# A gated relational graph layer: normalising and turning the input tiles inside the first sweep, landing weights from another queue, and splitting u a tile earlier

## The reference

```
h = maximum(layernorm(x), 0)
u = h @ root + bias
for r in range(8):
    sums = segment_sum(h[src] * (type == r), dst);  cnt = segment_sum(type == r, dst)
    u = u + (sums / maximum(cnt, 1)) @ weight[r]
z = concatenate([u, h]) @ w_gate + b_gate
out = x + tanh(u) * z + h * (1 - z)
```

## Time and profile before

| | us |
|---|---|
| median of 3 runs | 1621.51 (1617.54 to 1622.1) |
| the profiled execution's own time | 1619.02 |
| its span | 1617.3 |
| PE busy | 1444.5 |
| DVE busy | 682.4 |
| ACT busy | 345.6 |
| POOL busy | 644.0 |

### The profile page before, as it was taken

How to read it: one execution, slowest core, us unless ns; L and a number is a source line. 1 busy time by engine, 2 the same in 40 slices (tenths; PEclk the granted TensorE clock), 3 DMA queues, 4 the chain that set the end, 5 groups by cost and what they waited for, 6 DMA issues and landing times.

```text
span 1617.3 us, 21089 instructions
## 1 busy us (share of the span) xinstructions
PE 1444.5 (89%) x6978; PEld 777.6 (48%) x6978; DVE 682.4 (42%) x1163; ACT 345.6 (21%) x426; POOL 644.0 (40%) x1021
## 2 busy tenths in 40 slices
PE   1476999789999998999999989999999999897797
PEld 0233454345556444544545544455554455554464
DVE  5314965755564233224323312432332334454555
ACT  6324213110201121121222102212212111222221
POOL 2311000368784445344444434434443445410343
PEclk9877999899999999999999999999999999999898
DMA  4441031102001733544464364364455447411465
GB/s 188 129 155 49 39 142 64 40 27 114 1 1 53 247 120 111 190 150 134 128 231 133 119 216 128 118 232 138 132 175 184 126 133 252 136 53 60 125 200 157
DMA packets 63442, 207.41 MB, mean 128 GB/s; under 512 B 12709, under 2 KB 13084, under 8 KB 63354
## 3 DMA queue, kind: packets, MB, share of 16 engines
q0 software_dynamic: 28224, 81.95, 16.9%
q1 hardware_dynamic: 22458, 78.10, 14.2%
q10 hardware_dynamic: 12672, 46.14, 7.7%
HBM read 170.67 MB, written 56.32 MB: 140 GB/s over the span
## 4 chain that ended last, share of the span: by engine, by line
PE 75%; DVE 8%; DMA 5%; issue 4%; ACT 3%; POOL 2%; SPq 1%; ACTq 0%; POOLq 0%; DVEq 0%
PE ps L932 61%; PE ps L873 10%; DMA reg<-y_rows,idx 3%; DMA W<-in_x_dram 2%; PE ps L861 2%; DVE W L587 1%; PE ps L863 1%; DVE W L702 1%; DMA out_dram<-W 1%; ACT reg L437 1%; DVE sd L545 1%; PE ps L904 1%; ACT W L416 1%; POOL reg L335 1%; ACT yhl L505 1%
## 5 line engine op out<-in xcount | busy, mean ns | idle before, releaser
L932 PE MATMUL ps<-W,hT 128*128 128x512 f16 (+2 forms) x5280 | 1194.8, 384 | 0.0
L932 PEld LDWEIGHTS ps<-W,hT 128*128 128x128 f16 (+2 forms) x5280 | 582.7, 112 | 545.4 <-issue 22.8
L676 DVE SCALAR_TENSOR_TENSOR yhl<-ps,yhl 128x1024 f16<-128x1024 f32 x80 | 97.9, 1224 | 464.7 <-ACT yhl L505 464.7
L360 POOL DMA_INDIRECT reg<-y_rows,idx x196 | 220.3, 1124 | 155.8 <-POOL idx L357 125.9
L505 ACT ACTIVATE yhl<-ps 128x1024 f16<-128x1024 f32 x80 | 81.9, 1023 | 858.4 <-PE ps L932 858.4
L335 POOL TENSOR_SCALAR reg<-iota_t,ework 125x128 f16<-125x128 f16 x160 | 144.6, 911 | 207.6 <-DVE inv L649 175.5
L873 PE MATMUL ps<-reg,onehot 128*125 x784 | 196.4, 392 | 22.2 <-POOL onehot L367 17.0
L367 POOL TENSOR_SCALAR onehot<-iota_d,dcol 128x125 f16<-128x125 f16 x180 | 115.6, 642 | 106.4 <-DMA reg<-y_rows,idx 101.2
L356 POOL COPY dcol<-edge_dst 128x1 f32 x196 | 44.1, 225 | 250.4 <-PE ps L876 244.6
L873 PEld LDWEIGHTS ps<-reg,onehot 128*125 x784 | 100.7, 140 | 79.0 <-issue 28.8
L426 ACT ACTIVATE W<-W,wsc 128x1024 f16<-128x1024 f32 x88 | 96.5, 1140 | 97.9 <-PE ps L932 85.3
(11 more groups left out here) (126 smaller groups left out, 682.0 us busy)
## 6 DMA issues: line engine op xcount, KB each, us to landing
y_rows<-yhl SPq DMA_DIRECT2D x72, 512.0 KB
W<-in_L_gnn_weight_dram ACTq DMA_DIRECT2D x64, 512.0 KB, 8.7
W<-in_L_gnn_w_gate_dram ACTq DMA_DIRECT2D x16, 512.0 KB, 9.1
reg<-in_x_dram SPq DMA_DIRECT2D x9, 512.0 KB, 4.3
hs_rows<-reg SPq DMA_DIRECT2D x9, 512.0 KB, 5.2
zh_rows<-reg SPq DMA_DIRECT2D x10, 448.0 KB
W<-zh_rows SPq DMA_DIRECT2D x10, 448.0 KB
W<-hs_rows SPq DMA_DIRECT2D x10, 448.0 KB
```

The costliest lines, as they stand in the source:

```text
L360: pool.indirect_dma_start(out=G[:, b, :], out_offset=None, in_=y_rows[rel], in_offset=bass.IndirectOffsetOnAxis(ap=idx[:, b, :], axis=0), ...
L676: nc.vector.scalar_tensor_tensor(out=yhl[0:rows, m % 2, D:2 * D], in0=whole, scalar=2.0 ** -Y_BITS, in1=yhl[0:rows, m % 2, 0:D], op0=ALU.mult,
L932: last = nc.tensor.matmul(ps[0:rows, b + half, :], hT[:, v_h, k, n0:n0 + rows], Wh[:, HOME[w][k], v_w, half * HC:(half + 1) * HC], start=( ...
```

## The change

1. **Tiles three ahead, one per product.** `LEAD = 3`. Only tiles 0, 1 and 2 are normalised ahead of sweep 0; tile j+3 is normalised during product 0.j (on ACT ahead of its wait for that product), and tile j+2 is turned in the middle of product 0.j, for j from 1 on. DVE takes the statistics and moves the turned tile ahead of the evacuation. `scan_part` moves from behind products 3, 4, 5, 6 to behind 2, 4, 6, 7, POOL's memsets for it behind `split_low`. At the start, tile 2's normalisation stands ahead of the conversion of the first weight.
2. **SP lands weights.** All weights but slices 4 to 7 of the first land through SP's queue; weight w+1 when all products of sweep w-1 are done, that is one product sooner. ACT's four come at once, ahead of its wait for the constants, and a one-element square root loads ACT's table early.
3. **The first peek is shared.** ACT sums slices 0 to 3, DVE takes the maximum of slices 4 to 7 (`first_peek`).
4. **u is split a tile sooner.** `TURN0` goes from product 2 of gate_h to product 3; the splitting stays in its slots. So a tile is split a whole product ahead of its turning.

The diff, without the new buffer and semaphore:

```diff
@@ -58,8 +58,11 @@
-    TURN0 = slot(W_GH, 2)
-    assert all(AGG_AT[NG - NJ + j] <= 2 * (TURN0 - 1 + j) + 1 for j in range(NJ))
+    TURN0 = slot(W_GH, 3)
+    assert all(AGG_AT[NG - NJ + j] <= 2 * (TURN0 - 2 + j) + 1 for j in range(NJ))
...
+    LEAD = 3
@@ -221,22 +225,30 @@
+            def land(w, k0, k1):
+                for k in range(k0, k1):
+                    sp.dma_start(W[:, LAND[w][k], :], weight_slice(w, k)).then_inc(s[f"w_landed{k}"], 16)
...
             load_x(0)
+            land(0, 0, 2)
             load_x(1)
+            land(0, 2, 4)
             sp.dma_start(dst_i, dst.rearrange("(p c) -> p c", p=EP)).then_inc(s["edges_loaded"], 16)
...
             sp.dma_start(src_i, src.rearrange("(p c) -> p c", p=EP)).then_inc(s["edges_loaded"], 16)
-            for i in range(2, 4):
+            for i in range(2, LEAD + 2):
                 load_x(i)
...
                 for j in range(NJ):
-                    if w == 0:
-                        for i in range(2 * j + 4, 2 * j + 6):
-                            if i < NJ:
-                                load_x(i)
-                            if i - 2 < NJ:
-                                store_h(i - 2)
+                    if j == 0:
+                        if w:
+                            sp.wait_ge(s["gemm_done"], slot(w, 0))
+                        land(w + 1, 0, KT)
+                    if w == 0 and j + LEAD < NJ:
+                        if j + LEAD + 2 < NJ:
+                            load_x(j + LEAD + 2)
+                        store_h(j + LEAD)
                     if slot(w, j) == slot(1, 0):
@@ -245,6 +257,8 @@
                             s[f"y_stored{m % 2}"], 16)
+            sp.wait_ge(s["gemm_done"], slot(W_GH, 0))
+            land(W_GU, 0, KT)
             sp.wait_ge(s["evac"], slot(W_ROOT + 1, 0))
@@ -324,9 +338,9 @@
             for i in range(2, NJ):
-                if i % 2 == 0:
-                    scan_factors(i // 2 - 1)
                 split_low(i)
+                if i <= SQ + 1:
+                    scan_factors(i - 2)
@@ -405,14 +419,14 @@
         def _(act):
-            def land(w):
-                for k in range(KT):
+            def land(w, k0, k1):
+                for k in range(k0, k1):
                     act.dma_start(W[:, LAND[w][k], :], weight_slice(w, k)).then_inc(s[f"w_landed{k}"], 16)
...
                 if k >= 2:
-                    act.wait_ge(s["peeked"], w * KT + k - 1)
+                    act.wait_ge(s["peeked"], max(w * KT - 4, 0) + k - 1)
                 nc.scalar.activation(W[:, HOME[w][k % 2], :], W[:, LAND[w][k], :], ACT.Abs,
@@ -467,18 +481,19 @@
-            act.wait_ge(s["consts"], 8)
-            land(0)
+            land(0, 4, KT)
+            act.wait_ge(s["consts0"], 3)
+            nc.scalar.activation(warm[:, :], ones_f[:, 0:1], ACT.Sqrt)
             norm(0)
             norm(1)
-            turn_out(0)
-            for k in range(KT):
+            for k in range(4):
                 peek(0, k)
-            turn_out(1)
+            for i in range(2):
+                turn_out(i)
+            norm(2)
             for k in range(KT):
                 high_weights(0, k)
-            norm(2)
-            norm(3)
+            turn_out(2)
             for w in range(NW):
@@ -493,9 +508,10 @@
                     if w == 0:
-                        for i in range(2 * j + 2, 2 * j + 4):
-                            if i < NJ:
-                                turn_out(i)
+                        if j + LEAD < NJ:
+                            norm(j + LEAD)
+                        if 1 <= j and j + LEAD - 1 < NJ:
+                            turn_out(j + LEAD - 1)
                     act.wait_ge(s["gemm_done"], t + 1)
@@ -504,21 +520,15 @@
                                              ACT.Copy, scale=2.0 ** -Y_BITS).then_inc(s["y_hi"], 1)
-                    if w == 0:
-                        for i in range(2 * j + 4, 2 * j + 6):
-                            if i < NJ:
-                                norm(i)
                     if w + 1 < NW:
-                        if j == 0:
-                            land(w + 1)
                         if j in (2, 3):
...
                                 high_weights(w + 1, k)
-                    if 0 <= t + 1 - TURN0 < NJ:
-                        u_high(t + 1 - TURN0)
+                    if 0 <= t + 2 - TURN0 < NJ:
+                        u_high(t + 2 - TURN0)
@@ -567,9 +577,17 @@
-                dve.wait_ge(s["peeked"], (w + 1) * KT)
+                dve.wait_ge(s["peeked"], (w + 1) * KT - 4)
+                if w == 0:
+                    dve.wait_ge(s["peeked_first"], KT - 4)
                 step(nc.vector.tensor_reduce(wtop[:, 0:1], wsum[:, w, :], AX.X, ALU.max))
                 nc.vector.tensor_scalar(wspread[:, :], ones_f[:, :], wtop[:, 0:1], None, ALU.mult).then_inc(s["wtop_ready"], 1)
...
+            def first_peek(k):
...
+                dve.wait_ge(s[f"w_landed{k}"], 16)
+                nc.vector.tensor_reduce(wsum[:, 0, k:k + 1], W[:, LAND[0][k], :], AX.X, ALU.max,
+                                        apply_absolute_value=True).then_inc(s["peeked_first"], 1)
@@ -745,15 +763,16 @@
             edge_keys()
-            turn_out(0)
-            turn_out(1)
+            for k in range(4, KT):
+                first_peek(k)
+            for i in range(2):
+                turn_out(i)
             dve.wait_ge(s["consts"], 8)
...
             weight_scale(0)
+            stats_of(2)
             for k in range(KT):
                 low_weights(0, k)
-            stats_of(2)
-            stats_of(3)
             turn_out(2)
@@ -770,18 +789,16 @@
                         u_out(jj)
+                    if w == 0:
+                        if j + LEAD < NJ:
+                            stats_of(j + LEAD)
+                        if 1 <= j and j + LEAD - 1 < NJ:
+                            turn_out(j + LEAD - 1)
                     evacuate(w, j)
...
                         finish_tile(j)
-                    if w == 0:
-                        for i in range(2 * j + 4, 2 * j + 6):
-                            if i < NJ:
-                                stats_of(i)
-                        for i in range(2 * j + 3, 2 * j + 5):
-                            if i < NJ:
-                                turn_out(i)
-                        if 3 <= j <= 6:
-                            scan_part(j - 3)
+                    if w == 0 and j in (2, 4, 6, 7):
+                        scan_part((2, 4, 6, 7).index(j))
                     if t == TOTALS:
@@ -802,9 +819,9 @@
                         add_group(g)
-                    if 0 <= t + 1 - TURN0 < NJ:
-                        row_scale(t + 1 - TURN0)
-                        u_low(t + 1 - TURN0)
+                    if 0 <= t + 2 - TURN0 < NJ:
+                        row_scale(t + 2 - TURN0)
+                        u_low(t + 2 - TURN0)
@@ -908,14 +925,12 @@
             weight_max(0)
+            turn_h(2)
             for w in range(NW):
...
                     if w == 0:
-                        for i in range(2 * j + 2, 2 * j + 4):
-                            if i < NJ:
-                                turn_h(i)
                         pe.wait_ge(s["hT_hi"], j + 1)
@@ -941,6 +956,8 @@
                         if k == 3:
+                            if w == 0 and 1 <= j and j + LEAD - 1 < NJ:
+                                turn_h(j + LEAD - 1)
                             for g in AGG.get(2 * t, ()):
```

More of the change, by code:

```diff
@@ L126, in gated_rgcn_preln @@
         ltile = sb("ltile", [NG, P], BF16)
+        warm = sb("warm", [P, 1], F32)
         held = sb("held", [P, 2 * R], F32)
@@ L175, in gated_rgcn_preln @@
             "lnT_hi", "lnT_lo", "hT_hi", "hT_lo", "dve_step",
-            *(f"w_landed{k}" for k in range(KT)), "peeked", "wtop_ready", "wall_ready", "wscale_ready", "w_hi", "w_lo",
+            *(f"w_landed{k}" for k in range(KT)), "peeked", "peeked_first", "wtop_ready", "wall_ready", "wscale_ready", "w_hi", "w_lo",
             "factors_ready", "scan_ready", "totals_done", "ltile_ready", "bounds_done", "bounds_ready",
```

## The result

| us | before | after |
|---|---|---|
| median | 1620.33 (1617.54 to 1622.1, 4 runs) | 1543.05 (1540.62 to 1544.17, 4 runs) |
| profiled execution, span | 1619.02, 1617.3 | 1540.62, 1538.9 |

The account below looks back on a forecast made before the run. PE was taken to fill most of the span, with time to win at both ends: front 47.5, gate_h 19.5, gate_u 8.5, less 1, is 74.5 us off 1619.02, 1544.5; median 2.5 above, 1547, range 1530 to 1566.

Parts of the forecast that it names:

- First weight's scale, 29.2: At the start, weight 0's scale stays ready at 29.2 us, no gain; bounds 4 us sooner, 5 later.
- that conflict at the maxima: At the start, POOL's second subtraction might hold up DVE's four maxima; the scale would then come 2 us later.
- P0 = 48: Front: product 0.0 ends at 48 us instead of 64.2, 16 us won.
- Stalls in the sweep, 2.9, 8 and 6: Sweep 0: PE loses 2.9 us for tile 6, 8 for tile 8 and 6 ahead of the totals.
- Middle, -1: Between the ends: sooner landing of weights is hidden; the late bias row of gate_h loses 1 us.
- up to 11: gate_h's first evacuation comes up to 11 us late, its bias row queued behind eight weight slices on SP.
- Stores behind weights: Rival: each sweep's tile 0 store lands behind 4.2 MB of weights on SP, kernel slower, 1630 us; chance 0.03.
- gate_h, 19.5: In gate_h, waits for u's low half, slowed products and one turn go: 19.5 us won, bounds 13 and 22.
- gate_u, 8.5: In gate_u, a 4.2 us wait replaces 9.74 and the second turn ends sooner: 8.5 us won, bounds 3 and 10.
- longer-sweep rival: Rival: in sweep 0 all nine products take some 14 us as late pieces put off the next: 1562 us; chance 0.14.
- nothing at the back: Rival: DVE or z's loads bind, gate_h's gain stays half and gate_u's 0: 1565 us; chance 0.08.
- TensorE-bound rival: Rival: in sweep 0 DVE keeps ahead, half of 21 us between 148 and 169 is kept: 1536 us; chance 0.15.

Follow-up runs that it names:

- Experiment 5: Changed kernel with x tiles 0 and 1 and the edges ahead of weight 0's slices 0 to 3 in SP's queue: median 1537.26 us.
- Experiment 3: Changed kernel, but ACT lands weights 1 to 10 again, behind product w.0, instead of SP ahead of it: median 1545.85 us.
- experiment 4: Changed kernel, but SP lands weights 1 to 10 one product later, behind product w.0: median 1547.78 us.
- experiments 1 and 2: 1: changed kernel, u split a tile later again, median 1568.61 us; 2: kernel before, only u's split a tile sooner, median 1591.69 us.

## Why the prediction held, step by step

The mechanism was right and the total 4 us off. That it is so near is in part luck: the middle gave 8.5 us more than forecast, the two ends together 4.6 less.

- **First weight's scale, 29.2:** 32.6, inside the bounds. Two terms: the edges landed at 19.0, not 15, as x's second tile, the edges and the slices shared the queue and the DMA engines; and POOL's second subtraction held the cast, 1.7 us. I had looked for that conflict at the maxima. It came at a cast with one SBUF input. The Trainium skill (SBUF — State Buffer, Who interferes with whom) counts casts and `tensor_scalar` among what can contend as well, in a mode that uses both ports; the held cast agrees, but no row shows its mode. The maxima ran at 1.15 each with POOL idle, so the half on `tensor_reduce` was not put to the test. Experiment 5 shows the order in the queue to be worth 4.3 us of scale.
- **P0 = 48:** 53.3. 3.4 of the 5.3 is the scale. The last low half ends 16.8 us behind the scale, just as worked out, with POOL's hold of the first (2.21 instead of 1.28 us, which makes 10.91 of 9.98). The other 1.9 is TensorE, which ends 4.0 behind the last low half, not 2: its first ten matmuls took some 0.42 us each instead of 0.217.
- **Stalls in the sweep, 2.9, 8 and 6:** 2.4 (1.80 + 0.60), 5.1 (4.92 + 0.19) and 6.0, at the products named. Their rows name ACT's move of the tile before, which stands behind this tile's normalisation on ACT; the low half, which the forecast went by, is what ends each of the first two. The sum left out the lower clock behind the first: that half product took 7.03 us. The second was mis-sized: TensorE asked for tile 8 at 119.4 instead of 112.8, and its low half came at 125.5, 4.5 later than worked out. So of the 5.3 us 3.2 arrive at sweep 1: 173.2 for 170. Front won: 44.3, forecast 47.5.
- **Middle, -1:** the step that failed. It gave 5.7 up to gate_h's start (and 1.8 more to the start of gate_h.2). I took landing a product sooner for hidden, as PE never waits for a weight. But 4.2 MB in some 12 us compete with POOL's gathers, and PE does wait for one-hot rows. Experiment 3 shows some 6 us that hang on who lands and when; experiment 4 shows the bias row's part in the timing and makes it likely that who lands is the rest. In the kernel before, POOL waited over 6 us for a gather four times (6.9 the longest), each time while ACT's landing ran. Beside the one issued at 934.90 it waited 6.34, and behind that PE 4.59, its longest:

```profile
939.86 1.11 POOL L360 DMA_INDIRECT reg<-y_rows,idx  x1 [0.78 <-POOL idx L357]
947.31 0.61 POOL L367 TENSOR_SCALAR onehot<-iota_d,dcol 128x125 f16<-128x125 f16 x1 [6.34 <-DMA reg<-y_rows,idx]
```

  The bias row held its evacuation 9.1 us (1292.03 is 19.7 behind the product's start, before it was 10.6), inside the "up to 11" worked out. It cost nothing; a product later it costs about 5.
- **Stores behind weights:** tile 0's store did land later (up to 8.1 us from issue to landing, against a median of 3.0 for all), with no wait behind it. A slice took 11.4 us at the median, 8.7 before. The Trainium skill's ring order (DMA: Bandwidth & Descriptors, Queues, rings and completion order) agrees with the late bias row; that it would cost the kernel its gain no run shows.
- **gate_h, 19.5:** 18.1 (70.0 us between the ends of gate_h less 51.9 between the starts of gate_h.2). No wait for u's low half; one for one-hot rows (2.38) is new.
- **gate_u, 8.5:** 8.4. The stall for ACT's move is 5.23, forecast 4.2, the half product behind it 7.29. The loads moved as worked out: against the end of gate_h, ACT is at tile 3's h 8.6 us sooner and at tile 9's 8.4 (1464.02 and 1525.73).
- The longer-sweep rival is out, since only the named products stall; "nothing at the back" is out by experiments 1 and 2; the TensorE-bound rival would have needed the three stalls hidden.

## What to carry to other kernels

Marks that every variant passes turn one total into stretches: the back was 216.9 and 216.4, or 190.5 and 190.1, which settles what part 4 is worth. They also show when a gain of 2 or 3 us lies in a stretch that the edit doesn't touch. When a chain's tiles come late, look first at how early the consumer asks: moving one small product by half a slot gave 7.65 us, while moving 10 us scans about gave nothing. A transfer "nobody waits for" still has a price if its bytes run beside gathers that somebody waits for.

## What was unexpected in the hardware

- A DVE cast or `tensor_scalar` with one SBUF input was held until POOL's two-operand instruction ended: 1.90 for 0.23 us, 2.05 for 0.24. Both had started 0.3 us behind POOL's; a `tensor_scalar` that started together with it (15.41, experiment 5) took its 0.24.
- DVE's product of two SBUF operands took 3.28 instead of 1.24 us when POOL's instruction started just before it; taking TensorE's wait away made this the case for all ten.
- Behind the five stalls of TensorE named here in the changed kernel (1.80, 4.92, 5.96, 2.38 and 5.23 us) the next product or half took 1.6 to 1.9 us longer (12.12 and 7.29 above), while the granted clock stood at its lower level of 1.2 GHz (0.50 of 2.4). So a wait can cost more than its own length. Not every wait does: behind one of 2.59 us at 431.33 the clock stayed at its upper level. Windows of the changed kernel around the totals (PE busy, clock, DMA share, GB/s):

```profile
161.00:164.00 3.00, 2.99 (x8) 0.50 0.00 0
164.00:167.00 3.00, 3.00 (x14) 0.94 0.44 175
167.00:172.00 5.00, 5.00 (x25) 1.00 0.00 0
```
